# The first attention's first steps issued between the pieces of its setup's last product

## The reference, cut to what matters

```python
x = x + _L0_xattn_ref(_layernorm(x, axis=-1), ctx_768, ...)   # 16 heads of 64
# inside, for the context's 73 keys and, separately, its 4 others:
s = jnp.einsum('bhid,bhjd->bhij', q, k) * SCALE
p = jax.nn.softmax(s, axis=-1)
o = jnp.einsum('bhij,bhjd->bhid', p, v)
return out @ Wo + bo + _lora(out, o_down, o_up, o_alpha)
```

## Time and profile before

| | |
|---|---|
| median of 3 runs | 889.2 us (887.99 to 891.41) |
| the profiled execution | 886.54 us, of which the span of the core 884.7 us |
| mean granted TensorE clock | 0.976 |
| PE busy | 819.0 us, 93% |
| DVE busy | 658.4 us, 74% |
| ACT busy | 486.3 us, 55% |
| POOL busy | 253.6 us, 29% |

### The profile page before, as it was taken

The page is one execution under the profiler, slowest core; times in us unless marked ns, Lnnn a source line. Parts: engine busy times, 40 slices in busy tenths (PEclk is TensorE's granted clock), DMA queues, the critical chain, the costliest instruction groups (busy, mean ns, idle before and its releaser), DMA issues. The chain is left out here.

```text
span 884.7 us, 17781 instructions
## 1 busy us (share of the span) xinstructions
PE 819.0 (93%) x6093; PEld 757.0 (86%) x6093; DVE 658.4 (74%) x1307; ACT 486.3 (55%) x1022; POOL 253.6 (29%) x216
## 2 busy tenths in 40 slices
PE   8988999998799999999999999978799968999977
PEld 6876899998489999999999999965698845989867
DVE  3884899997776347888888878967688777776657
ACT  3652333333375566777777777753355543645653
POOL 8410322322005530233344233230122201522530
PEclk9999999999999999999999999998899997999999
DMA  8990000000403248677666778726000051524325
GB/s 304 294 299 14 2 1 0 1 1 1 155 1 131 99 157 318 218 223 219 221 219 219 224 223 255 239 25 190 1 1 1 0 173 60 157 98 126 107 84 181
DMA packets 60067, 115.92 MB, mean 131 GB/s; under 512 B 8483, under 2 KB 45957, under 8 KB 53221
## 3 DMA queue, kind: packets, MB, share of 16 engines
q1 hardware_dynamic: 48420, 97.48, 33.2%
q0 software_dynamic: 9408, 15.53, 7.3%
q10 hardware_dynamic: 2176, 2.10, 0.7%
HBM read 84.29 MB, written 30.79 MB: 130 GB/s over the span
## 5 line engine op out<-in xcount | busy, mean ns | idle before, releaser
L143 PE MATMUL e_ps_h<-e_xh,e_w1h 128*128 128x256 f32 (+1 forms) x496 | 141.3, 285 | 0.0
L144 PE MATMUL e_ps_h<-e_xl,e_w1h 128*128 128x256 f32 (+1 forms) x496 | 138.7, 280 | 0.0
L145 PE MATMUL e_ps_h<-e_xh,e_w1l 128*128 128x256 f32 (+1 forms) x496 | 138.2, 279 | 0.0
L2000 POOL DMA_INDIRECT accumulated<-m_yo,m_token x39 | 79.5, 2039 | 192.8 <-ACT m_yo L2140 163.6
L905 POOL TENSOR_TENSOR at_pr<-at_pr,at_inv 128x1168 f32<-128x1168 f32 (+2 forms) x48 | 58.7, 1238 | 222.9 <-DVE at_inv L837 222.9
L145 PE MATMUL e_ps_o<-e_w2h,e_hl 128*128 128x256 f32 x440 | 122.0, 277 | 0.4 <-issue 0.4
L143 PE MATMUL e_ps_o<-e_w2h,e_hh 128*128 128x256 f32 x440 | 122.2, 278 | 0.0
L144 PE MATMUL e_ps_o<-e_w2l,e_hh 128*128 128x256 f32 x440 | 121.8, 277 | 0.0
L2120 ACT ACTIVATE e_hf<-e_ps_h,e_b1s 128x256 f32<-128x256 f32 (+1 forms) x248 | 98.2, 447 | 37.8 <-PE e_ps_h L145 33.3
L144 PEld LDWEIGHTS e_ps_h<-e_xl,e_w1h 128*128 128x128 f32 x496 | 94.3, 190 | 0.0
L145 PEld LDWEIGHTS e_ps_h<-e_xh,e_w1l 128*128 128x128 f32 x496 | 94.3, 190 | 0.0
(11 more groups left out here) (384 smaller groups left out, 2289.1 us busy)
## 6 DMA issues: line engine op xcount, KB each, us to landing
e_w1s<-in_m_w SPq DMA_DIRECT2D x24, 1024.0 KB
e_w2s<-in_m_w SPq DMA_DIRECT2D x24, 1024.0 KB, 6.8
slots_in<-zero SPq DMA_DIRECT2D x20, 258.0 KB, 9.5
e_xin<-slots_in SPq DMA_DIRECT2D x16, 258.0 KB
last_slots_in<-zero SPq DMA_DIRECT2D x14, 258.0 KB, 8.0
d_xin<-last_slots_in SPq DMA_DIRECT2D x10, 258.0 KB
d_results<-last_results SPq DMA_DIRECT2D x10, 256.0 KB, 5.0
as_wk<-in_a_wk SPq DMA_DIRECT2D x2, 1024.0 KB, 9.2
```

What stands on the lines that cost most here:

```text
L143: nc.tensor.matmul(out, lh, rh, start=start, stop=False)
L144: nc.tensor.matmul(out, lh, rl, start=False, stop=False)
L145: return nc.tensor.matmul(out, ll, rh, start=False, stop=stop)
L2000: nc.gpsimd.indirect_dma_start(out=g.acc[a], out_offset=bass.IndirectOffsetOnAxis(ap=token[:, n, a:a + 1], axis=0), in_=yo[:, q, a, :], in ...
```

## The change

B's ten pieces go round four banks (`as_ps_b` twice, then `as_ps_a` twice), so TensorE waits for piece i-4 instead of i-2. Between the pieces stand the first steps of the attention, called through an object `Begun`: T0 behind piece 3, S0 and T1 behind piece 4, S1 and T2 behind piece 7. DVE normalises tiles 0 and 1 ahead of piece 0's subtraction, and does the maxima, shift and sums of tile 0 and the maxima and shift of tile 1 between the subtractions; ACT loads the exponential's table ahead of piece 0's copy and does tile 0's exponential behind piece 5's copy. POOL no longer waits for the end of the setup. The dummy matmuls of the first attention are gone. The second attention is made without `Begun`.

```diff
+    b_bank = lambda i: ps_b[:, i % 2] if i % 4 < 2 else ps_a[:, i % 2].rearrange("p (a d) -> p a d", d=D)
...
         for i, (b, c0, nch) in enumerate(b_items):
-            wait(pe, s_blo, i - 1)
+            wait(pe, s_blo, i - 3)
+            if i in (2, 3):
+                pe.wait_ge(s_alo, DK * (G - 1) + i - 1)
             for k in range(c0, c0 + nch):
-                o = ps_b[:, i % 2, k - c0, :]
+                o = b_bank(i)[:, k - c0, :]
...
             last.then_inc(s_b, 1)
+            if i == 3:
+                begun.transpose_first(pe)
+            if i == 4:
+                pe.wait_ge(s_alo, DK * G)
+                begun.scores(pe, 0)
+            if i == 7:
+                begun.scores(pe, 1)
...
         deviation.dve(dve)
+        begun.normalise_first(dve)
         for i, (b, k, nch) in enumerate(b_items):
+            if i == 5:
+                begun.shift_first(dve)
+            if i == 7:
+                begun.sum_first(dve)
+            if i == 8:
+                begun.shift_second(dve)
             dve.wait_ge(s_bhi, i + 1)
...
+            if i == 2:
+                begun.low_first(dve)
+            if i == 8:
+                begun.low_third(dve)
...
         deviation.act(act)
+        a.preload_act_table(ACT.Exp)
         for i, (b, k, nch) in enumerate(b_items):
             act.wait_ge(s_b, i + 1)
-            a.copy(Bh[:, b, k:k + nch, :], ps_b[:, i % 2, 0:nch, :]).then_inc(s_bhi, 1)
+            a.copy(Bh[:, b, k:k + nch, :], b_bank(i)[:, 0:nch, :]).then_inc(s_bhi, 1)
+            if i == 3:
+                begun.high_first(act)
+            if i == 5:
+                begun.exp_first(act)
+            if i == 8:
+                begun.high_third(act)
...
+            def step(t, q):
+                static = isinstance(t, int)
+                if not begun or not static or t > 0:
+                    ahead(t, q)
+                if static and t <= 0 and not begun:
                     warm(nc, g, ps_o[:, 0:D], 4 if t == 0 else 6 if L.lora else 2)
...
+        def shift_first():
+            shift(-1, 1)
+            low_x(1, 1)
+            normalise(2, 0)
...
     def gpsimd(pool):
-        stage_over(pool, after)
+        if not begun:
+            stage_over(pool, after)
```

More of the change, by code:

```diff
@@ L288, in finish, with attach, first_setup @@
         dve.wait_ge(s_r, n + 5)
-def first_setup(nc, ctx, own, g, L, w, sem, prepare):
+class Begun:
+    def attach(self, tensor, vector, scalar):
+        self.transpose_first = lambda pe: tensor(pe, -1)
+        self.scores = lambda pe, t: tensor(pe, t)
+        self.normalise_first = lambda dve: vector(dve, 0)
+        self.low_first = lambda dve: vector(dve, 1)
+        self.shift_first = lambda dve: vector(dve, 2)
+        self.sum_first = lambda dve: vector(dve, 3)
+        self.high_first = lambda act: scalar(act, 0)
+        self.exp_first = lambda act: scalar(act, -1)
+        self.shift_second = lambda dve: vector(dve, 4)
+        self.low_third = lambda dve: vector(dve, 5)
+        self.high_third = lambda act: scalar(act, 2)
+def first_setup(nc, ctx, own, g, L, w, sem, prepare, begun):
     T = f"as{L.n}_"
@@ L492, in vector @@
         deviation.dve(dve)
+        begun.normalise_first(dve)
         for i, (b, k, nch) in enumerate(b_items):
-            dve.wait_ge(s_bhi, i + 1)
-            v.tensor_tensor(Bl[:, b, k:k + nch, :], ps_b[:, i % 2, 0:nch, :], Bh[:, b, k:k + nch, :], ALU.subtract).then_inc(s_blo, 1)
+            if i == 5:
[4 more added lines that the diff above has]
+                begun.shift_second(dve)
+            dve.wait_ge(s_bhi, i + 1)
+            v.tensor_tensor(Bl[:, b, k:k + nch, :], b_bank(i)[:, 0:nch, :], Bh[:, b, k:k + nch, :], ALU.subtract).then_inc(s_blo, 1)
+            if i == 2:
+                begun.low_first(dve)
+            if i == 8:
+                begun.low_third(dve)
     def scalar(act):
@@ L682, in second_setup, with attention @@
     return Stage(before.sync, tensor, gpsimd, vector, scalar, (s_blo, len(b_items)))
-def attention(nc, ctx, g, L, sem, after, deviation):
+def attention(nc, ctx, g, L, sem, after, deviation, begun=None):
     T = f"at{L.n}_"
@@ L727, in steps, with tensor @@
                     body(i + 1, (lo + 1) % 2)
-    def tensor(pe):
-        stage_over(pe, after)
+    def tensor(pe, first=None):
         def transpose_x(t, q):
@@ L738, in make, with ahead @@
         def make(b_s, b_o):
-            def step(t, q):
+            def ahead(t, q):
                 static = isinstance(t, int)
@@ L757, in step @@
                     transpose_x(t + 2, q)
-                if static and t <= 0:
+            def step(t, q):
[3 more added lines that the diff above has]
+                if static and t <= 0 and not begun:
                     warm(nc, g, ps_o[:, 0:D], 4 if t == 0 else 6 if L.lora else 2)
@@ L774, in step, with vector @@
                     last.then_inc(s_pt, 1)
-            return step
+            return ahead if first is not None else step
+        if first is not None:
+            make(0, 0)(first - 1, (first - 1) % 2) if first >= 0 else transpose_x(0, 0)
+            return
+        stage_over(pe, after)
         pe.wait_ge(s_pad, 1)
-        transpose_x(0, 0)
+        if not begun:
+            transpose_x(0, 0)
         h = NT // NB
-        steps(pe, make(0, 0), [(-1, 1), (1, 3), (3, h - 1)])
+        steps(pe, make(0, 0), [(0 if begun else -1, 1), (1, 3), (3, h - 1)])
         steps(pe, make(1, 0), [(h - 1, h + 1)])
         steps(pe, make(1, 1), [(h + 1, NT - 3), (NT - 3, NT - 1), (NT - 1, NT + 1)])
-    def vector(dve):
-        stage_over(dve, after)
+    def vector(dve, first=None):
         def normalise(t, q):
@@ L798, in low_x, with shift @@
                                     ALU.subtract).then_inc(s_xlo, 1)
-        def step(t, q):
+        def shift(t, q):
             static = isinstance(t, int)
@@ L818, in step, with total @@
                 last.then_inc(s_sub, 1)
-            if not static or t + 2 < NT:
+        def total(t, q):
+            wait(dve, s_exp, t + 2)
+            wait(dve, s_pn, t + 1)
+            e = pr[:, 1 - q, 0:L.cols].rearrange("p (h j) -> p h j", h=H)
+            for i, (j0, j1) in enumerate(L.segments):
+                nc.vector.tensor_reduce(su[:, :, i:i + 1], e[:, :, j0:j1], AX.X, ALU.add).then_inc(s_sum, 1)
+            wait(dve, s_sum, NS * (t + 2))
+            nc.vector.reciprocal(inv[:], su[:]).then_inc(s_inv, 1)
+        def step(t, q):
+            static = isinstance(t, int)
+            started = begun and static and t == 0
+            if not started:
+                shift(t, q)
+            if not static or t + 2 < NT and not started:
                 low_x(t + 2, q)
@@ L830, in step @@
             if not static or t + 1 < NT:
[L831 to L837, removed]
+                total(t, q)
             if not static or 0 <= t < NT:
@@ L854, in aggregate, with pad_and_normalise @@
                 nc.vector.bn_aggr(g.mv[:, t, :], g.stats[:, t, :]).then_inc(s_aggr, 1)
[L856 to L860, removed]
+        def pad_and_normalise():
+            nc.vector.memset(pr[:, :, L.cols:], 0.0).then_inc(s_pad, 1)
+            normalise(0, 0)
+            normalise(1, 1)
+        def shift_first():
+            shift(-1, 1)
+            low_x(1, 1)
+            normalise(2, 0)
+        if first is not None:
+            (pad_and_normalise, lambda: low_x(0, 0), shift_first, lambda: total(-1, 1),
+             lambda: shift(0, 0), lambda: low_x(2, 0))[first]()
+            return
+        stage_over(dve, after)
+        if not begun:
+            pad_and_normalise()
+            low_x(0, 0)
+        steps(dve, step, [(0 if begun else -1, 1), (1, 3), (3, NT - 3), (NT - 3, NT - 1), (NT - 1, NT + 1)])
         dve.wait_ge(s_bn, NT)
@@ L863, in vector, with scalar @@
         dve.wait_ge(s_aggr, NT)
-    def scalar(act):
-        stage_over(act, after)
+    def scalar(act, first=None):
         def high_x(t, q):
@@ L873, in step @@
             static = isinstance(t, int)
-            if not static or t + 2 < NT:
+            if not static or t + 2 < NT and not (begun and t == 0):
                 high_x(t + 2, q)
@@ L893, in step @@
                     nc.scalar.copy(ph[:, cs], probs_t[:, cs]).then_inc(s_phi, 1)
-        nc.scalar.preload_act_table(ACT.Exp)
-        high_x(0, 0)
-        steps(act, step, [(-1, 1), (1, 3), (3, NT - 3), (NT - 3, NT - 1), (NT - 1, NT + 1)])
+        if first is not None:
+            high_x(first, 0) if first >= 0 else step(-1, 1)
+            return
+        if not begun:
+            stage_over(act, after)
+            nc.scalar.preload_act_table(ACT.Exp)
+            high_x(0, 0)
+        steps(act, step, [(0 if begun else -1, 1), (1, 3), (3, NT - 3), (NT - 3, NT - 1), (NT - 1, NT + 1)])
     def gpsimd(pool):
-        stage_over(pool, after)
+        if not begun:
+            stage_over(pool, after)
         def step(t, q):
@@ L911, in gpsimd @@
             step(i + 1, 1)
```

(7 more changed lines are left out.)

## The result

| | before | changed |
|---|---|---|
| median | 888.6 us (887.71 to 891.41, 4 runs) | 878.34 us (873.55 to 885.92, 4 runs) |
| profiled execution | 886.54 us, span 884.7 | 876.45 us, span 874.6 |
| mean granted clock, profiled | 0.976 | 0.974 |

The ratio is 0.9865, with an interval of 0.9825 to 0.9906: faster by 0.9% to 1.8%. (The quotient of the two medians in the table, 0.9885, lies inside it.) The changed kernel run again in another session gave 878.71 us and 0.9851 (0.9804 to 0.9897).

The account below looks back on a forecast made before the run. TensorE paces the tile loop, so an earlier S2 is kept. Four banks gain 1.8 us and moving the run-in into the product 7.9, together 9.7; 889.2 - 9.7 = 879.5 us, range 876.5 to 883.3.

Parts of the forecast that it names:

- The place: Start of S2, tile 2's scores: 9.7 us earlier, at about 86.3 instead of 96.00 us, kept by the loop.
- The wait ahead of S0: New TensorE wait between piece 4 and S0, for tile 0's normalised parts: 0.2 us.
- the one ahead of P0: New TensorE wait behind piece 9, until DVE's subtractions let all ten pieces leave: 2.0 us.
- 13.5 + 1.5: The product's length without waits: 13.5 us of matmuls plus 1.5 us for 16 matmuls at the low clock.
- The margins: Covers costed at nothing: S1 behind piece 7 has 1.3 us to spare; POOL's multiply for P0 needs 9.8 against 13.1.
- Four banks, 1.8 us: Inside the product: waiting for the piece four before removes all waits between pieces, gaining 1.8 us.
- The dummies cost nothing by being gone: In the run-in before the loop: the dummy matmuls stood in waits, so removing them costs 0 us.
- Rival 1: One clock fall behind the wait ahead of P0 slows P0 and S2: gain 8.1 us, 881.1 us; chance 0.37.
- taking 0: Price of the clock behind the wait ahead of P0: bounds 0 and 1.55 us, 0 taken, odds nearly even.
- The row that decided for 0: Clock row between 220 and 226 us: TensorE idle 1.9 us in all, yet the clock stayed at 1.00.
- Rivals 2 and 3: 2: DVE or ACT order blocks steps, no gain, 889 us (0.06); 3: clock falls repeatedly into the loop, 895 (0.03).
- The rule set against the change: Skill's rule: brief pauses while going round PSUM banks make the clock swing; the product would fall again and again.

Follow-up runs that it names:

- the better version: The changed kernel with P0 waiting for nine of ten pieces and eight dummy matmuls in the 2.44 us wait before piece 0: 877.1 us, ratio 0.9831.
- the profile with two banks: The changed kernel with its pieces going round two banks again instead of four: ratio 0.9892 to the kernel before.
- before, no dummies: The kernel before without the dummy matmuls of the first attention: ratio 1.0025.
- without tile 1's part: The changed kernel with S1, T2, tile 1's maxima and shift and tile 2's low part behind the product again: ratio 0.9920 to the kernel before.

## Why the prediction was right

**The place.** S2 was to start 9.7 us earlier, at 86.3, and the loop was to keep it. It started 10.2 us earlier, at 85.77 (0.2 of it because piece 0 began earlier in that execution), and the profiled executions differ by 10.1 us. The median, 878.3, lies 1.2 us under the forecast of 879.5.

**The terms.** The wait ahead of S0 was 0.21 us for 0.2, the one ahead of P0 1.95 for 2.0, S0 and S1 3.53 and 3.44 us for 3.55. Other terms were off and in part cancel. P0 occupies TensorE for 1.06 us (84.71 to 85.77), not the 1.25 of its row, and of each pair of transposes a part of the 0.38 lies under the next matmul: T0, T1 and T2 take 0.6 us together, not 1.14. Against that the product itself, the stretch less the moved steps and the waits, took 15.5 us, not 13.5 + 1.5. The margins held: S1 found tile 1's low part ready 0.95 us early (75.49 against 76.44; 1.3 forecast), and GpSimd was done 2.8 us before P0 (3.3 forecast).

**The parts at an even clock.** With the clock at 1.00 throughout, the kernel before takes 34.01 us from piece 0 to S2, and the changed one would take 23.87 + 0.92 = 24.8 (the better version with its earlier P0 taken back): 9.2 us less. The four banks are 2.3 of that, tile 1's place 2.6; the rest, 4.3 us, is left for tile 0's steps by subtraction, as no run took those back alone. The other 0.8 us of the 10.06 that the stretch lost lie with the clock, which slowed S0 before and not after.

**Four banks, 1.8 us.** Right in kind: 2.3 at the full clock, and within the changed kernel 1.2 from S0 to S1 and 0.33 ahead of piece 3. The estimate subtracted the low clock from the product's length in one profile; a slower product also waits less for its banks, which that hides: with two banks 3.4 us at the low clock made T0 start only 0.8 us later (18.86 us behind piece 0 against 18.03).

**The dummies cost nothing by being gone.** The reason given was not complete. In the old order the ones ahead of S1 stood in a wait and yet were worth 2.7 us, because they held the clock. They can go because the change removes that wait. A wait ahead of P0, where the other four stood, is still there: 1.95 us, without a dummy in it now, and the clock fell behind it in two of three profiles. Dummies in that wait were not tried.

**Rival 1, chance 0.37.** It is not a rival so much as the other face of the same kernel: of two profiles of the changed kernel one kept its clock behind the wait and one lost it, at 1.6 us for 1.55, and the profile with two banks, which has the same wait, lost it as well. So taking 0 was luck for the first profile, and the runs, which spread from 873.55 to 885.92 us, can't tell the forecast of 879.5 from rival 1's 881.1. The row that decided for 0 was misread, too: the 1.9 us of idle time between 220 and 226 us are one wait of 1.49 us and the first 0.4 us of the next, so none of them was as long as the 2.0:

```profile
221.85 0.36 PE L143 MATMUL at_ps_o<-B_high,at_ph 128*128 128x256 f32 x1 [1.49 <-DVE at_pl L841]
```

**Rivals 2 and 3** did not occur: S2 came 10.2 us earlier, and between 64 and 84.7 us the granted clock was 1.00. That says little on short waits, though, since four banks took them away: between piece 0 and S1 the changed kernel has one wait, 0.21 us. The kernel before with dummies ahead of piece 0 tests them better: two banks, a wait of 1.09 us for a bank, and a granted clock of 1.00 over the whole product. The rule set against the change, of the Trainium skill, "TensorE: Matmul & The Clock Gate", section "A second HAM failure mode: psum-queue depth-cycling", did not decide here: going round two banks with these pauses did not lower the clock. In the stretch of all these profiles every fall came behind a wait of 1.94 us or more (the 2.44 us ahead of piece 0 among them), and not every such wait brought one.

## What to carry to other kernels

Where one stage drains and the next fills, count TensorE's idle time between them as a sum of single waits, and look for banks that the first stage has left: the first steps of the next can stand between the last pieces of the old one, until another engine's chain is without a gap, as VectorE's is here ahead of P0. After such a move ask whose completion the next step really needs; P0 needed nine pieces, not ten. A wait of TensorE costs its length and here sometimes the clock behind it, so price both, think of the dummies that an earlier version put there, and compare edits at an even clock before judging one of 2 us.

## What the runs showed of the hardware

The same wait lowers TensorE's clock in one execution and not in another: 1.95 us ahead of P0 (1.00 behind it in one profile of the changed kernel, 0.54 over the next 3.7 us in the other), and 1.95 and 1.19 us ahead of S0 (low in the profile of before, not in that of its copy with dummies ahead of piece 0). Length alone does not order them: 1.95 us ahead of P0 lost the clock, 2.16 us ahead of S2 kept it (before, no dummies), 2.23 us ahead of S2 lost it (without tile 1's part). The runs spread accordingly: over ten runs of the changed kernel the mean granted clock went from 0.978 (872.86 us) to 0.967 (885.92 us), so that the 13 us between them are about 20 us more at the low clock ((0.978 - 0.967) x 2 x 880 = 19). At the price of S0 before, 1.55 us for 3.4 us at the low clock, that makes about 9 of the 13 us (an estimate). So the clock accounts for most of the spread; what the rest is, and in which stage each run lost its clock, the runs without a profile don't show. The Trainium skill, in "TensorE: Matmul & The Clock Gate", Part 1, says of a kernel's start that one and the same kernel meets a different number of slow matmuls from run to run. The two profiles of the changed kernel show the same kind of thing in the middle of a kernel, with 3.42 and 7.94 us at the low clock in the same stretch.
